# A four-layer gated cross-attention kernel: a filled gap behind the second attention, and shorter norms, quantisers and way out

## The reference, cut to what matters

```python
x = x + jnp.tanh(g_xattn[0]) * _L0_xattn_ref(_layernorm(x, axis=-1), ctx_1024, ctx_1024, ...)
x = x + jnp.tanh(g_ffn[0]) * _L0_ffn_ref(_layernorm(x, axis=-1), ...)      # quantised, 3 matrices
x = x + jnp.tanh(g_xattn[1]) * _L1_xattn_ref(_layernorm(x, axis=-1), ...)  # 16 heads, window
x = x + jnp.tanh(g_ffn[1]) * _L1_ffn_ref(_layernorm(x, axis=-1), ...)      # 16 experts + shared
x = x + jnp.tanh(g_xattn[2]) * _L2_xattn_ref(ctx_1024, _layernorm(x, axis=-1), ...)
x = x + jnp.tanh(g_ffn[2]) * _L2_ffn_ref(_layernorm(x, axis=-1), ...)      # quantised, 2 matrices
x = x + jnp.tanh(g_xattn[3]) * _L3_xattn_ref(ctx_1024, ctx_1024, _layernorm(x, axis=-1), ...)
x = x + jnp.tanh(g_ffn[3]) * _L3_ffn_ref(_layernorm(x, axis=-1), ...)      # 8 experts
```

## Time and profile before

| what | us |
|---|---|
| median of three runs (lowest, highest) | 823.86 (820.6, 825.62) |
| the profiled execution's own time | 820.25 |
| its span | 818.4 |
| PE busy | 727.2 |
| DVE busy | 623.2 |
| ACT busy | 434.1 |
| POOL busy | 348.1 |
| mean granted clock of TensorE | 0.945 of full speed |

### The profile page before, as it was taken

How to read it: one execution, slowest core, us unless ns; L and a number is a source line. 1 busy time by engine, 2 the same in 40 slices (tenths; PEclk the granted TensorE clock), 3 DMA queues, 4 the chain that set the end, 5 groups by cost and what they waited for, 6 DMA issues and landing times.

```text
span 818.4 us, 15421 instructions
## 1 busy us (share of the span) xinstructions
PE 727.2 (89%) x5504; PEld 467.2 (57%) x5504; DVE 623.2 (76%) x1304; ACT 434.1 (53%) x739; POOL 348.1 (43%) x283
## 2 busy tenths in 40 slices
PE   4699999997876878977999999997899999898997
PEld 4587877776544465753455555563346666653443
DVE  4679999998888684877555666658789999616786
ACT  2656676767475352425554545432127677743673
POOL 0564556661523421540778777730241211102464
PEclk9889999999999777999999999998859999999999
DMA  7267766632414523207023332006726678102520
GB/s 209 76 200 245 258 185 222 188 121 77 99 54 135 168 62 97 87 10 180 1 81 98 111 97 83 1 15 105 149 48 140 110 125 157 52 2 64 181 78 12
DMA packets 51510, 89.74 MB, mean 110 GB/s; under 512 B 17522, under 2 KB 35642, under 8 KB 50962
## 3 DMA queue, kind: packets, MB, share of 16 engines
q1 hardware_dynamic: 51442, 88.83, 40.2%
HBM read 63.29 MB, written 25.52 MB: 109 GB/s over the span
## 4 chain that ended last, share of the span: by engine, by line
PE 30%; DVE 16%; ACT 3%; POOL 2%; issue 2%; DVEq 0%; POOLq 0%; ACTq 0%
DVE arena L2550 10%; PE ps L1181 9%; PE ps L1171 6%; PE ps L1350 3%; PE ps L1286 2%; PE ps L1364 2%; DVE arena L1926 2%; PE ps L1275 2%; POOL arena L1848 2%; PE ps L1258 1%; ACT arena L1675 1%; PE ps L1217 1%; PE ps L1329 1%; PE ps L1187 1%; PE ps L786 1%
## 5 line engine op out<-in xcount | busy, mean ns | idle before, releaser
L2550 DVE TENSOR_REDUCE arena<-ps 112x1 f32<-112x500 f32 x192 | 114.6, 670 | 7.7 <-PE ps L1258 7.6
L1848 POOL TENSOR_TENSOR arena<-arena 125x448 f32<-125x448 f32 x96 | 109.3, 1139 | 24.5 <-ACT arena L1634 20.0
L1675 ACT ACTIVATE arena<-ps 125x896 f32<-125x896 f32 x96 | 87.2, 917 | 24.8 <-PE ps L1275 24.7
L1926 DVE TENSOR_TENSOR arena<-ps,arena 128x448 f32<-128x448 f32 (+7 forms) x139 | 80.5, 612 | 24.5 <-ACT arena L1703 8.0
L1181 PE MATMUL ps<-arena 125*128 125x448 f32 (+1 forms) x208 | 97.2, 548 | 2.0 <-ACT arena L1634 1.5
L1634 ACT ACTIVATE arena<-arena,kbias 125x448 f32<-125x448 f32 x96 | 63.6, 667 | 65.4 <-DVE arena L1926 47.9
L1926 DVE TENSOR_TENSOR arena<-ps,rn 125x448 f32<-125x448 f32 x96 | 59.2, 618 | 47.0 <-PE ps L1171 41.1
L861 PE MATMUL ps<-w_k2h,arena 128*125 128x512 f16 x288 | 69.9, 394 | 11.8 <-ACT arena L1432 10.6
L1171 PE MATMUL ps<-arena 128*125 128x448 f16 (+3 forms) x312 | 76.5, 354 | 1.3 <-DVEq L1937 1.1
L1171 PEld LDWEIGHTS ps<-arena 128*125 128x125 f16 (+1 forms) x312 | 40.1, 133 | 54.8 <-issue 41.8
L1432 ACT ACTIVATE arena<-ps 125x512 f32<-125x512 f32 x96 | 55.4, 598 | 12.3 <-PE ps L861 9.2
(11 more groups left out here) (325 smaller groups left out, 1489.8 us busy)
## 6 DMA issues: line engine op xcount, KB each, us to landing
arena<-in_ctxT SPq DMA_DIRECT2D x8, 750.0 KB, 9.1
d_cln<-arena SPq DMA_DIRECT2D x8, 750.0 KB
d_clnT<-arena SPq DMA_DIRECT2D x8, 750.0 KB
d_k<-arena SPq DMA_DIRECT2D x24, 250.0 KB
d_v<-arena SPq DMA_DIRECT2D x24, 250.0 KB
arena<-d_clnT SPq DMA_DIRECT2D x8, 750.0 KB
arena<-in_ctx SPq DMA_DIRECT2D x8, 672.0 KB
arena<-d_cln SPq DMA_DIRECT2D x8, 672.0 KB
```

Source lines behind the costliest of these rows:

```text
L1675: act.activation(p3[t % 2].rearrange("p (k h) q -> p k (h q)", k=2), ps[0:KP, 2 * (t % 2):2 * (t % 2) + 2, 0:8 * S], ACT.Exp).then_inc(l3_ ...
L1848: ins = pool.tensor_tensor(psum2[p][0:rows], psum2[p][0:rows], pexp[(t + p) % 2][0:rows], ALU.add)
L1926: return dve.tensor_tensor(out, a, b, op)
L2550: dve.tensor_reduce(mx3[bn % 2][:, u % 2, u % 8 // 2, u // 8:u // 8 + 1], ps[0:TT, max_bank_of(bn, u), 0:500], AX.X, ALU.max).then_inc(l3_ ...
```

## The change

It makes eight edits:

1. PE: in front of the last `turn_probs1`, nine products that nobody reads, into bank 1, once all scores are read.
2. DVE: the reciprocal of the key norms is split into 480 elements ahead of `normalise1(2)` and 288 ahead of `normalise1(3)`.
3. PE: the first expert's product waits for the remainder of its input only at its third product, and the order of the three products changes for all experts.
4. DVE: the residual of expert 16 stands before that of POOL's sum.
5. ACT: a one-element exponential ahead of the third attention's loop. POOL: unit 23's remainder stands behind the norm's power.
6. PE and DVE: the way out of the third attention writes four banks, and DVE copies each tile and takes its statistics while PE works on the next.
7. DVE: norms without a gain subtract the mean in one `tensor_tensor` of 512 features while POOL works, and multiply in a second one behind it.
8. DVE: the quantiser folds 1/127 into the bound, drops the product by 127, and makes the results' scales later.

```diff
@@ second attention, PE
             for i in range(NT):
+                if i == NT - 1:
+                    pe.wait_ge(l1_sr, NT)
+                    keep_clock(9, 1)
                 turn_probs1(i)
@@ experts of layer 1, PE
-                pe.wait_ge(ex_split, 3 if g < 2 else g + 2)
+                if e:
+                    pe.wait_ge(ex_split, 3 if g < 2 else g + 2)
+                else:
+                    pe.wait_ge(ex_split, 2)
+                    pe.wait_ge(ex_hi, 3)
...
-                    for n, (w, a) in enumerate(((0, 0), (0, 1), (1, 0))):
+                    for n, (w, a) in enumerate(((0, 0), (1, 0), (0, 1))):
+                        if e == 0 and m == 0 and a:
+                            pe.wait_ge(ex_split, 3)
@@ way out of the third attention, PE
-                    mm = pe.matmul(ps[0:TT, 0, D * t:D * t + D], ctxT[:, h, TT * t:TT * t + TT], m2[:, h, :],
+                    mm = pe.matmul(ps[0:TT, t, 0:D], ctxT[:, h, TT * t:TT * t + TT], m2[:, h, :],
                                    start=(h == 0), stop=(h == H8 - 1))
-            mm.then_inc(product, 1)
+                mm.then_inc(l2_out, 1)
+            pe.nop().then_inc(product, 1)
@@ ACT, ahead of the third attention's loop
+            act.activation(exs[0][0:1, 0:1], tg[0:1, 0:1], ACT.Exp)
@@ POOL
-            remainders(22, 23)
+            remainders(22)
...
             rsqrt()
+            remainders(23)
@@ DVE, layernorm
                     ch.sync()
+                else:
+                    ch.link(tt(dst, src, over(lnmv[:, :, 0], [TT, NT, D]), ALU.subtract))
...
-                        ch.step(dve.tensor_scalar(dst[:, t, :], src[:, t, :], lnmv[:, t, 0:1], lnrs[:, t:t + 1],
-                                                  ALU.subtract, ALU.mult))
+                else:
+                    ch.step(tt(dst, dst, over(lnrs, [TT, NT, D]), ALU.mult))
@@ DVE, quantise
-                ch.link(dve.tensor_scalar(acol[:, 0, :], acol[:, 0, :], 1e-5, None, ALU.max))
+                ch.link(dve.tensor_scalar(acol[:, 0, :], acol[:, 0, :], 1e-5, 1.0 / 127.0, ALU.max, ALU.mult))
                 ch.link(dve.reciprocal(acol[:, 1, :], acol[:, 0, :]))
-                ch.link(dve.tensor_scalar(acol[:, 1, :], acol[:, 1, :], 127.0, None, ALU.mult))
-                for row, m in scales:
-                    ch.step(dve.tensor_scalar(acol[:, row, :], acol[:, 0, :], 1.0 / 127.0, mw[0:TT, m:m + 1],
-                                              ALU.mult, ALU.mult))
+                def results_scales():
+                    for row, m in scales:
+                        ch.step(dve.tensor_scalar(acol[:, row, :], acol[:, 0, :], mw[0:TT, m:m + 1], None, ALU.mult))
+                    ch.sync()
@@ DVE, second attention
-                if i == 2:
+                if i > 1:
...
-                    ch.step(dve.reciprocal(rn_flat, rn_flat))
+                    some = slice(0, 480) if i == 2 else slice(480, B * KT * H8)
+                    ch.step(dve.reciprocal(rn_flat[:, some], rn_flat[:, some]))
@@ DVE, end of the experts of layer 1
-            dve.wait_ge(ex_acc, E1)
-            residual(5, y2)
             for e in range(E1 - 2, E1):
                 dve.wait_ge(ex_dn, e + 1)
                 residual(5, ps[0:TT, 6 + e % 2, :].rearrange("p (t n) -> p t n", t=NT))
+                if e == E1 - 2:
+                    dve.wait_ge(ex_acc, E1)
+                    residual(5, y2)
+            for _ in range(2):
                 dve.nop().then_inc(ex_w, 1)
                 dve.nop().then_inc(ex_acc, 1)
@@ DVE, way out of the third attention
+            for t in range(NT):
+                dve.wait_ge(l2_out, t + 1)
+                ch.link(dve.tensor_copy(y[:, t, :], ps[0:TT, t, 0:D]))
+                ch.step(dve.bn_stats(lnst[:, t, :], y[:, t, :]))
+            ch.sync()
             product_in.next()
-            ch.link(dve.tensor_copy(y.rearrange("p t n -> p (t n)"), ps[0:TT, 0, :]))
             signal(l3_free)
-            layernorm(y, y, 1e-5, "L2_ow", "L2_ob")
+            layernorm(y, y, 1e-5, "L2_ow", "L2_ob", counted=True)
```

19 lines of the change are left out of this document (12 added, 7 removed).

## The result

The changed kernel took 811.11 us (median of 4 runs, 808.96 to 812.83) beside 823.01 us of the kernel before (4 runs, 820.6 to 825.62): ratio 0.9859, 95% interval 0.9836 to 0.9883. The change is 1.4% faster. The forecast was 816.1 us, with a range from 812.0 to 820.5, so the time lies 0.9 us under the range. In the profiled execution it took 809.71 us, span 807.8.

A forecast was written before the change was run, and what follows sets the result against it. No engine was the bound: PE or DVE paces the long loops, and each edit shortens a seam between them. Terms summed to 7.75 us, taken off the median 823.86 for 816.1 us; range 812.0 to 820.5.

The forecast's parts named there:

- Attention's end, 3.2 us: End of the second attention: nine unread products and the cut reciprocal save 3.2 us, with last values' products nearly half at full clock.
- Rival A: Second attention's end: clock kept through the gap, lost again some 5 us later; whole kernel 813.5 to 818.5 us; chance 0.5.
- the ceiling of 5.2 us: Second attention's end: everything runs at full clock, saving 5.2 us together.
- The middle of 2.5: Second attention's end: clock kept through the gap, half clock from the start of the last values' products; 2.5 us saved.
- the floor: Second attention's end: low clock despite or during the unread products, cut reciprocal gives nothing; -1.5 us.
- The norm ahead of the experts, -0.3 us: Norm before layer 1's experts: earlier power gains, but later loads make expert group 2 up to 0.3 us late; -0.3 us.
- Exponential, 1.3: Third attention's start: the table load at 389.60 moves ahead of the loop, beside PE's products; 1.3 us saved.
- Norms and quantisers ahead of 267.8, 0.35 in my sum: Ahead of the second attention: norm at 264 saves 0.25 us, ending about when POOL does; quantiser at 251 saves 0.1.
- Norms at 578 and 742, 0.43 each: Norms ahead of the fourth attention and last experts: four scalings become one operation, nothing else on POOL; 0.43 us each.
- B: Full clock to the attention's end gives 2.0 us more there, 814.1 us in all; chance 0.2.
- C: Second attention's end: the clock is low despite the unread products; 819.3 us, or 820.8 at worst; chance 0.18.
- D: Moved remainder costs 2 us more, or the table load stays in the loop; 817.4 to 818.1 us; chance 0.08.

The follow-up runs named there:

- more filler: Changed kernel with six more unread products ahead of the last values' products and five ahead of the last turn_out1: attention's end 9.76 us; 812.57 us, ratio 0.9895.
- the one with the seams alone: Kernel before with only the residual's place, the exponential ahead of the loop and the tile-wise way out (edits 4, 5, 6): ratio 0.9937.
- the kernel with norms and quantisers alone: Kernel before with only the norms without gain and the quantisers changed (edits 7 and 8): ratio 0.9984.

## Why the prediction was wrong

It was too cautious: 7.75 us of saving against 11.3 to 11.9 measured, and a range that ended 0.9 us above the measured time. Three terms of the sum failed and one thing the range had left out; they are named below. Together the terms were 0.8 us too small. The larger part of the miss, about 3 us, stands in no stage of the traces, and its cause stays open.

**Attention's end, 3.2 us: right in kind and size.** The table's mean is 2.75; traces have 2.4 or 4.2 us by where the clock falls. Rival A's mechanism, clock kept through the gap and lost at the last values' products, is what the timeline of after shows, and the ceiling of 5.2 us was reached with more filler. The middle of 2.5 was what three of the changed kernel's four traces had, and four of the eight with these edits; my 3.2 lies between the two cases, and no trace had it. That the cut reciprocal is worthless without the filler was said in the floor, and measured (15.03 us).

**The norm ahead of the experts, -0.3 us: about 0.** The size was nearly right and the reason was not. From the output product's use to the first copy behind the norm 6.84 us pass, as before (6.85): what the moved remainder freed, the longer power (1.38, not 1.01 us) and the multiplication beside the remainder (1.48, not 0.69) took back. The first expert's product then starts 0.46 us earlier (8.33 us behind the output product's use instead of 8.79), and at the last expert's product nothing of that is left (45.18 and 45.19 where the clock was the same). But it was not the load of group 2 that took it. SP's issue came 9.30 us behind the output product's use instead of 7.78, and still DVE's split has no idle time in front of it in any of the four traces; where the clock was the same it began 17.24 to 17.30 us behind it, and 17.41 to 17.43 before. I had written that no idle time there would make the term too low, and so it is. The split took 1.95 to 2.01 instead of 0.95 us beside POOL's sum in three of four traces, and 1.92 in one of six of before.

**End of the experts, 0.85: right.** The last residual starts 1.62 us behind the last product's start instead of 2.57: 0.95. The norm behind it starts 0.74 earlier, and with about 0 for the norm ahead of the experts that is the 0.75 between the shortest stages of the table, against my 0.55.

**Exponential, 1.3: 2.0.** This is the first step that failed. I read the load at 389.60 as the table load of the third attention. ACT's timeline of before has four, one for each pass of the loop:

```profile
389.60 1.28 ACT L1634 ACT_TABLE_LOAD   x1 [3.66 <-DVE arena L1926]
426.63 1.28 ACT L1634 ACT_TABLE_LOAD   x1 [0.82 <-DVE arena L1926]
464.19 1.28 ACT L1634 ACT_TABLE_LOAD   x1 [0.82 <-DVE arena L1926]
501.74 1.28 ACT L1634 ACT_TABLE_LOAD   x1 [0.82 <-DVE arena L1926]
```

With the exponential ahead of the loop all four are gone from it, in the changed kernel and in the one with the seams alone, and one load stands ahead of the loop; the kernel with norms and quantisers alone keeps the times of before. The first was worth 0.9 us at equal clock and each of the other three 0.37 on PE: from 440.9 to 500.0 PE's list took 59.10 us with and 58.73 without. That is 2.0 against 1.3. Between two traces without low clock there, 187.8 us from 369.5 to 557.3 became 184.8, and 1.0 of these 3.0 us is the way out's. So "none of the eight edits is inside a long loop" was wrong. The rule of the Trainium skill, "ScalarE: Activation LUTs", section "What ACT_TABLE_LOAD costs", that I had put beside it, a drain with the load and 2.66 us in all, is not borne out: PE's idle time in front of the first values' product fell by 1.27 us. At the second load 2.12 us pass from the end of ACT's instruction ahead of it to the start of the one behind it, the load and the wait for DVE together.

**Way out, 1.0: right.** From the end of the way out's products to the quantiser's row maximum 8.74 us pass instead of 9.72. The table's row of 1.37 holds two of the table loads beside it, and a shift of DVE against PE at its start.

**Norms and quantisers ahead of 267.8, 0.35 in my sum: 1.34.** The second step that failed. I wrote that at 264 "POOL holds on until 265.91 whichever instruction DVE has there". In three of the changed kernel's four traces it doesn't: DVE's one operation of 1.52 us gets in between POOL's two remainders, which together take 2.58 (before: 2.88 and 2.10), and PE's transposes start 4.7 us behind the statistics instead of 5.6, 0.9 us saved. The fourth trace is as I wrote:

```profile
262.36 2.09 POOL L1771 TENSOR_TENSOR arena<-arena 128x500 f16<-128x500 f32 x2
262.49 2.51 DVE L1938 TENSOR_TENSOR arena<-arena 112x512 f32<-112x512 f32 x1 [0.97 <-POOL arena L1755]
```

There the transposes start 5.7 us behind the statistics, and the norm saves nothing. Of six traces of other kernels with this form of the norm, two have the first outcome and four the second. What decides is not shown. The quantiser at 251 gave 0.5 instead of 0.1 us: I had priced the product that went by its undisturbed 0.17 us for all three, and here it met POOL's remainder. From the timeline of before:

```profile
251.53 0.88 DVE L1991 TENSOR_SCALAR arena<-arena 112x4 f32<-112x4 f32 x1
```

That the norm and the quantiser ahead of the first feed-forward part are hidden was right.

**Norms at 578 and 742, 0.43 each: 0.0.** The third step that failed, to the other side. "Beside the power (1.01 us, so it is hidden)" looked at DVE's time alone: the subtraction stretches POOL's power by 0.37 us, and that is nearly all of the 0.43 that the shorter multiplication saves. The Trainium skill, "GPSIMD Engine Reference", section "Key points", names two forms that meet POOL, DVE's 2-port fast modes and two SBUF inputs. The traces agree on two inputs: POOL's power took 1.38 us. Operations with one input met POOL too (2.50 instead of 0.87 us), but in which mode they ran no trace shows. Nor does the number of operands say who waits: the two-input multiplication, which started 0.13 us behind POOL's remainder, waited itself (1.48 to 2.51 instead of 0.69 us), while for the two-input subtraction, which started 0.17 us ahead of POOL's power, POOL waited.

**Quantisers at 558 and 566, 0.5: 0.7 to 0.9.** At the first, from the row maximum to PE's first transpose, 2.62 us instead of 2.96: 0.34, as forecast. The rest is at the second and in low stretches there; how it divides was not worked out.

**The range, which failed too.** In the traces the stages sum to 8.4 us. The three errors above (0.7 and 1.0 too little, 0.9 too much) add up to 0.8 us, about the 0.65 between that and my 7.75, and the smaller ones nearly cancel with what the last loop lost. That the sum came near what the stages show is in part luck. The range was made of the terms' bounds alone, and the time it was taken from was the median of three runs that spread over 5 us; the 29 runs beside the first experiments spread over 11. With the fourth run the median of before was 823.01 and not 823.86, and that alone is 0.85 of the 0.9 us by which the time lies under the range. Against the mean of 78 executions, 822.0, the reference was 1.9 us too high. Low stretches and other differences that come and go in unchanged code moved single executions by 4 us ahead of the first edit and by over 2 us in the last loop, within one kernel. None of that was in the range.

**Rivals.** B (full clock to the end) did not come by itself; when forced, it gave the attention its 2.8 us and the kernel nothing. C, D and E did not occur; the stretch behind 361.5 did cost the clock in several traces of both kernels, by 2.0 us at most in the stage to 394.6 (27.12 against 25.08 before), far from my 9.4 us.
